# The sum over wavelengths moves from VectorE to GpSimd, and GpSimd's queue is put in another order

## The reference

```python
scores = einsum('bhqd,bhkd->bhqk', Q * m, K * m) * SCALE   # m = cos(phase[w, h]), per wavelength w, head h
scores = scores * cos(KERR * scores * scores)              # KERR = 2.7e-12
attn = softmax(scores, axis=-1)
acc += einsum('bhqk,bhkd->bhqd', attn, V) * iw[w]          # over 16 wavelengths
...
x = layernorm(x + (acc / 16) @ Wo + bo)
gates = top-2 of softmax(x @ router_w + router_b) over 8 experts and a pass-through
x = layernorm(x + sum_e gates[e] * gelu(x @ w1[e]) @ w2[e] + gates[8] * x)
```

## Time and profile before

| | |
|---|---|
| median of 3 runs | 7535.9 us (7534.82 to 7537.15) |
| profiled execution | 7540.05 us, span 7538.4 us |
| mean granted TensorE clock | 0.939 of full speed |
| ScalarE (ACT) | 7184.6 us busy, 95% of the span |
| TensorE (PE) | 5560.1 us, 74% |
| VectorE (DVE) | 5456.0 us, 72% |
| GpSimd (POOL) | 44.4 us, 1% |
| exponentials L522 | 6979.3 us in 2048 instructions |
| reduction L773 | 64 instructions of about 1.9 us |

### The profile page before, as it was taken

One profiled execution on the slowest core, in us unless ns is written; L12 is line 12 of the kernel. 1 busy time (PEld: TensorE's weight loads), 2 busy tenths in 40 slices (PEclk: granted clock), 3 DMA queues, 4 the chain that ended last, 5 costly groups with the idle time before them and its releaser, 6 DMA issues.

```text
span 7538.4 us, 124074 instructions
## 1 busy us (share of the span) xinstructions
PE 5560.1 (74%) x43972; PEld 2013.9 (27%) x43972; DVE 5456.0 (72%) x9488; ACT 7184.6 (95%) x2227; POOL 44.4 (1%) x112
## 2 busy tenths in 40 slices
PE   6767767677777777777777777777777777777777
PEld 2222222222222222222222222222222222222225
DVE  4767677767777777777777777777777777777763
ACT  4999999999999999999999999999999999999992
POOL 0000000000000000000000000000000000000000
PEclk7999999999999999999999999999999999999998
DMA  2000000000000000000000000000000000000000
GB/s 57 4 4 4 2 4 4 3 3 9 28 25 28 17 26 23 19 28 19 29 28 16 25 28 16 26 28 16 28 30 17 26 27 14 28 17 26 27 12 34
DMA packets 40422, 151.80 MB, mean 20 GB/s; under 512 B 7969, under 2 KB 26273, under 8 KB 33441
## 3 DMA queue, kind: packets, MB, share of 16 engines
q1 hardware_dynamic: 39072, 142.13, 5.7%
q0 software_dynamic: 768, 1.57, 0.1%
HBM read 132.66 MB, written 11.01 MB: 19 GB/s over the span
## 4 chain that ended last, share of the span: by engine, by line
ACT 44%; issue 29%; PE 12%; DVE 8%; ACTq 6%; DMA 1%; DVEq 0%; POOLq 0%; SPq 0%; POOL 0%
ACT ring L522 43%; PE pv L593 8%; ACTq L517 4%; DVE scores L724 2%; DMA out<-tile_out 1%; DVE vprobs L747 1%; ACTq L518 1%; DVE tile_z L810 1%; PE sc L1042 1%; PE tr L1050 1%; PE sc L648 1%; DVE qt L718 0%; DVE tile_small L360 0%; DVE tile_small L359 0%; DVE tile_small L361 0%
## 5 line engine op out<-in xcount | busy, mean ns | idle before, releaser
L522 ACT ACTIVATE ring<-scores 128x4096 f32<-128x4096 f32 (+3 forms) x2048 | 6979.3, 3497 | 144.5 <-PE pv L593 109.3
L593 PE MATMUL pv<-ring,vh 128*32 128x512 f32 x31744 | 4010.8, 635 | 1702.1 <-ACT ring L522 1574.4
L593 PEld LDWEIGHTS pv<-ring,vh 128*32 128x32 f32 x31744 | 1003.7, 115 | 4350.8 <-ACT ring L522 2189.0
L754 DVE COPY numer<-pv 128x512 f32<-128x512 f32 x512 | 353.6, 691 | 1067.7 <-PE pv L593 1062.4
L747 DVE SCALAR_TENSOR_TENSOR vprobs<-vprobs,vrest 128x512 f32<-128x512 f32 x1536 | 1063.8, 693 | 52.3
L714 DVE TENSOR_REDUCE rowmax<-sc 128x1 f32<-128x1024 f32 x512 | 602.5, 1219 | 120.8 <-PE sc L556 120.8
L724 DVE COPY scores<-sc 128x1024 f32<-128x1024 f32 (+1 forms) x512 | 601.6, 1217 | 59.0 <-PE sc L575 58.4
L593 PE MATMUL pv<-vprobs,vh 128*32 128x512 f32 x1024 | 530.3, 599 | 0.0
L745 DVE TENSOR_TENSOR vprobs<-vprobs,vrest 128x512 f32<-128x512 f32 x512 | 354.7, 693 | 17.6
L741 DVE SCALAR_TENSOR_TENSOR vrest<-vpower,vrest 128x512 f32<-128x512 f32 x512 | 354.6, 693 | 17.6
L748 DVE SCALAR_TENSOR_TENSOR vprobs<-vprobs,vpower 128x512 f32<-128x512 f32 x512 | 354.5, 692 | 17.4
(11 more groups left out here) (156 smaller groups left out, 2408.2 us busy)
## 6 DMA issues: line engine op xcount, KB each, us to landing
tile_w<-in_L_ffn_w SPq DMA_DIRECT2D x48, 2048.0 KB, 7.6
qt<-q_scratch SPq DMA_DIRECT2D x256, 36.0 KB
kt_<-k_scratch SPq DMA_DIRECT2D x256, 36.0 KB
ring<-in_L_ffn_w SPq DMA_DIRECT2D x2, 2048.0 KB, 11.5
scores<-in_L_attn_x SPq DMA_DIRECT2D x4, 512.0 KB, 4.9
q_scratch<-qt SPq DMA_DIRECT2D x4, 512.0 KB, 3.9
k_scratch<-kt_ SPq DMA_DIRECT2D x4, 512.0 KB, 4.2
v_scratch<-vv SPq DMA_DIRECT2D x4, 512.0 KB, 3.5
```

The source lines that it names most:

```text
L522: nc.scalar.activation(ring[:, i % SLOTS, 0:cols], scores[:, bass.ds(n % 2, 1), half * CK:(half + 1) * CK, :].rearrange("p o k s -> p (o k ...
L593: last = nc.tensor.matmul(pv[g * VC:(g + 1) * VC, pair % 2, :], vh[:, buf, half * CK + k, :], probs, start=(half == 0 and k == 0), stop=(h ...
L754: nc.vector.tensor_copy(numer[:, pair, :], pv[:, pair, :]).then_inc(pv_read, 1)
```

## The change

The reduction of VectorE is removed. In its place GpSimd adds the 8 pairs of wavelengths of `parts` in a tree, in place (4 + 4, 2 + 2, 1 + 1), then the two wavelengths of the pair that is left into a new small tile `att_head`, and copies that into `att`; a semaphore wait stands between the steps. VectorE waits for `head_summed` ahead of the first write to `parts` of the next head, since the tree works in place. On GpSimd's queue a pair of heads n, n+1 is now: copy the values of head n+2, sum head n, store the tile and wait for it, copy the values of head n+3, sum head n+1. The loop's last round is written out, without copies.

```diff
@@ -123,6 +123,7 @@
         coef = sb("coef", [P, 32])
         parts = sb("parts", [P, W // 2, 8, 2, D])
         att = sb("att", [P, KT, E])
+        att_head = sb("att_head", [P, KT, D])
 
 
         tile_w = sb("tile_w", [P, NE * F])
@@ -194,7 +195,7 @@
         def pool_setup(pool):
             for started in (xT_ready, q_made, k_made, v_mm, v_made, peak_made, qkv_stored, probs_ready, tr_full,
                             tr_read, att_made, att_stored, gen_scores, gen_tr, ff_x1, ff_gelu, ff_expert,
-                            ff_added, ff_stored, tile_x1_made, tile_products, tile_added, tile_out_free):
+                            ff_added, ff_stored, tile_x1_made, tile_products, tile_added, tile_out_free, head_summed):
                 pool.sem_inc(started, START)
             nc.gpsimd.memset(numer[0:NH, :, :], 0.0).then_inc(edges_made, 1)
             nc.gpsimd.memset(vprobs[0:NH, :, :], 1.0).then_inc(edges_made, 1)
@@ -426,6 +427,7 @@
         pv_read = sem("pv_read")
         tr_full, tr_read = sem("tr_full"), sem("tr_read")
         norm_step = sem("norm_step")
+        head_step, head_summed = sem("head_step"), sem("head_summed")
 
         tile_in, tile_w1, tile_w2 = sem("tile_in"), sem("tile_w1"), sem("tile_w2")
         tile_attT_ready, tile_attT_made, tile_y = sem("tile_attT_ready"), sem("tile_attT_made"), sem("tile_y")
@@ -484,21 +486,45 @@
             pool.wait_ge(slot_free, NCH * (n - 1) + SLOTS)
             nc.gpsimd.tensor_copy(vh[:, buf, :, 0:D], vv[:, :, bass.ds((n % H) * D, D)]).then_inc(vh_ready, 1)
 
+        def sum_wavelengths(pool, n):
+            pool.wait_ge(tr_read, 4 * (n + 1) + START)
+            apart(pool)
+            for step, left in enumerate((4, 2, 1)):
+                nc.gpsimd.tensor_tensor(parts[:, 0:left], parts[:, 0:left], parts[:, left:2 * left], ALU.add).then_inc(head_step, 1)
+                pool.wait_ge(head_step, 3 * n + step + 1)
+                apart(pool)
+            nc.gpsimd.tensor_tensor(att_head[:, :, :], parts[:, 0, :, 0, :], parts[:, 0, :, 1, :], ALU.add).then_inc(head_summed, 1)
+            pool.wait_ge(head_summed, n + 1 + START)
+            pool.wait_ge(att_stored, 32 * (n // H) + START)
+            apart(pool)
+            nc.gpsimd.tensor_copy(att[:, :, bass.ds((n % H) * D, D)], att_head[:, :, :]).then_inc(att_made, 1)
+
         def pool_main(pool):
             pool.sem_inc(slot_free, SLOTS)
             pool.wait_ge(v_loaded, 16)
             nc.gpsimd.tensor_copy(vh[:, 0, :, 0:D], vv[:, :, 0:D]).then_inc(vh_ready, 1)
             nc.gpsimd.tensor_copy(vh[:, 1, :, 0:D], vv[:, :, D:2 * D]).then_inc(vh_ready, 1)
-            with pool.Fori(1, FIRST_PAIR) as i:
-                copy_values(pool, 2 * i, 0)
-                copy_values(pool, 2 * i + 1, 1)
-            with pool.Fori(0, PAIRS - FIRST_PAIR) as i:
-                copy_values(pool, 2 * (i + FIRST_PAIR), 0)
-                copy_values(pool, 2 * (i + FIRST_PAIR) + 1, 1)
+            with pool.Fori(0, FIRST_PAIR) as i:
+                copy_values(pool, 2 * i + 2, 0)
+                sum_wavelengths(pool, 2 * i)
+                copy_values(pool, 2 * i + 3, 1)
+                sum_wavelengths(pool, 2 * i + 1)
+
+            def tile_heads(i, last=False):
+                n = 2 * (i + FIRST_PAIR)
+                if not last:
+                    copy_values(pool, n + 2, 0)
+                sum_wavelengths(pool, n)
                 pool.wait_ge(tile_done, i + 1)
                 pool.dma_start(out_tiles[bass.ds(i, 1)].rearrange("o p e -> p (o e)"), tile_out[:, :]).then_inc(tile_stored, 16)
                 pool.wait_ge(tile_stored, 16 * (i + 1))
                 pool.sem_inc(tile_out_free, 1)
+                if not last:
+                    copy_values(pool, n + 3, 1)
+                sum_wavelengths(pool, n + 1)
+            with pool.Fori(0, PAIRS - FIRST_PAIR - 1) as i:
+                tile_heads(i)
+            tile_heads(PAIRS - FIRST_PAIR - 1, True)
 
         def scalar_main(act):
             act.preload_act_table(ACT.Exp)
@@ -763,15 +789,11 @@
                                     wl_wide[:, 2 * quad:2 * quad + 2, :, :].rearrange("p a t w -> p (a t w)"),
                                     ALU.mult).then_inc(norm_step, 1)
             dve.wait_ge(norm_step, 8 * n + 2 * quad + 2)
+            if quad == 0:
+                dve.wait_ge(head_summed, n + START)
             nc.vector.tensor_tensor(parts[:, 2 * quad:2 * quad + 2, :, :, :].rearrange("p a t w d -> p (a t w) d"), blocks[:, :, 0:D],
                                     coef[:, :].rearrange("p (g o) -> p g o", o=1).to_broadcast([P, 32, D]),
                                     ALU.mult).then_inc(tr_read, 1)
-
-        def sum_wavelengths(dve, n):
-            dve.wait_ge(tr_read, 4 * (n + 1) + START)
-            dve.wait_ge(att_stored, 32 * (n // H) + START)
-            nc.vector.tensor_reduce(att[:, :, bass.ds((n % H) * D, D)], parts[:, :, :, :, :].rearrange("p a t w d -> p t d a w"),
-                                    axis=AX.XY, op=ALU.add).then_inc(att_made, 1)
 
         def tile_part_one_vector(dve, i, step, then):
             if step == 0:
@@ -853,7 +875,6 @@
                     elif at == 15 and more:
                         exponentials(dve, n + 1, 0)
             normalise(dve, n, 3)
-            sum_wavelengths(dve, n)
 
         def vector_main(dve):
             for t in range(KT):
```

## The result

The changed kernel is slower: a median of 7591.5 us against 7537.2 us for the kernel before in the same series, a ratio of 1.0071 with a 95% interval of [1.0056, 1.0086]. The forecast was 7465 us in a range of 7448 to 7508.

The account below looks back on a forecast made before the run. ScalarE's stream of exponentials was taken to bound the kernel, so only its idle time could be gained: 7540.05 - 86.4 + 11.4 + 4.1 = 7469.2 us, less 4.15 from profiled execution to median, 7465.0 us; range 7448 to 7508.

Parts of the forecast that it names:

- its two gaps: ScalarE's idle places four and twenty exponentials into the even head of tile pairs: 86.4 and 20.0 us in all.
- the start gap: ScalarE's idle time four exponentials into a tile pair's even head, 23 of 24 pairs, 86.4 us, expected to go.
- GpSimd's wait goes in 23 pairs: At pair starts, copying values ahead of the tile's store ends TensorE's wait for GpSimd: -86.4 us.
- this place is clean, with 2.7 to 3 us in hand: At the pair start, nothing else was said to be late once the copies come early; slack 2.7 to 3 us.
- store latency: Pair-start stall read as GpSimd's wait for the tile's store to land, plus the slow clock after idling; 4.00 us at one boundary.
- The second gap, 11.4 us given back: ScalarE's idle time twenty exponentials into the even head grows to a mean of 1.1 us: 22 x 0.52 = 11.4 us lost.
- one of two exceptions: First and last tile pairs before the change lost 3.62 and 3.71 us at twenty exponentials; other 22 lost 0.54 to 0.60.
- Rival A: The stall moves to twenty exponentials, 3.6 us in every pair: 66.9 us given back, 7520 us; chance 0.20.
- The tree at 3.7 us, hidden by 31 us: GpSimd's sum of a head takes 3.7 us and costs nothing, since VectorE needs it only 31 us later.
- rival B: GpSimd's tree and VectorE's exponentials lock each other out of SBUF: 7646 us at 6 us a head; chance 0.04.
- The tail, +4.1 us: Behind the last head, GpSimd's store and tree end at 7374.5 instead of 7370.38: +4.1 us once, bounds +1.8 and +13.
- VectorE's 122 us are worth nothing: Removing 64 reductions of 1.91 us from VectorE gains nothing on ScalarE's stream, as VectorE then waited 2.61 us for TensorE.

Follow-up runs that it names:

- busy_and_cut: Changed kernel with TensorE's loop cut inside the odd head and 36 extra matmuls a pair in TensorE's idle time: 7456.2 us, 0.9894 of the kernel before.
- sum_only: Kernel before with only the tree sum on GpSimd, both copies of values still behind the tile's store: 7541.2 us, 1.0007.
- the last pair of runs: Changed kernel, TensorE's loop cut inside the odd head, router product and ScalarE's small exponential later; with tree 7428.0 us, with VectorE's reduction 7428.9 us.
- numer_first: Changed kernel with VectorE copying a pair's last numerators ahead of the tile's last layer norm: 7484.2 us, 0.9929 of the kernel before.
- loop_cut_moved: Changed kernel with TensorE's jump back moved between steps 3 and 4 of the odd head, where it waits for the GELU: 7536.6 us, 0.9997.
- before_two_pairs: Kernel before with TensorE's loop over pairs written out twice per round: 7556.8 us, 1.0026.

## Why the prediction was wrong

- *That ScalarE's stream bounds, and its two gaps are all there is to gain*: right in the main; without the start gap and with 21.1 us of the second it is 7456.2 us (`busy_and_cut`), and 7428 without either, with the router and its small exponential moved.
- *That GpSimd's wait goes in 23 pairs*: right. *That this gives 86.4 us, for "this place is clean, with 2.7 to 3 us in hand"*: this is the step that failed. Behind the wait lay TensorE's restart, 3.0 to 3.7 us in 22 pairs, and it was 9.7 us, not 86.4, that went. The trace of before had it in full view: the wait list has `PE pv L593 <- issue: 23.3, 7, 3.5`, seven times, once for every jump back in the 16 heads without a tile. The first pair, which has no gap, is entered from the loop ahead without a jump back; its missing gap was explained by the missing store. I took the free moment of an engine for the moment at which it could issue. The rest of the stall was also read too simply: "store latency" was 3.7 to 4.5 us beside the jump and 2.62 in the last pair, where there is none.
- *The second gap, 11.4 us given back*: its direction and its cause, the clock, were right, its size was not: 49.7 us, a mean gap of 2.9 us where 1.1 was put in. Slow batches were put in one pair of six, and came in 17 of 24. The last pair of before, where TensorE stood idle the shortest at the start (2.80 us) and the second gap was 3.71, was a sign of it; it was counted as one of two exceptions. Rival A had 66.9 us, at a chance of 0.20, and the worse half of it outside the range, but never beside start gaps that stay.
- *The tree at 3.7 us, hidden by 31 us*: right, 3.6 us from 7414.25 to 7417.82, and 3.9 with its waits inside the loop; VectorE's wait for it cost nothing, `sum_only` shows it. The factor of two of the Trainium skill ("GPSIMD Engine Reference", section Engine selection) had led to an estimate of 4.6 with the waits, which was less near. Without the waits the five instructions took 3.0 us together, between the 2.5 of my sum and the 3.4 by that factor. VectorE's exponentials did not get longer (L773, 692 ns, against 693 for the same line, L747, before), so rival B falls.
- *The tail, +4.1 us*: +1.8. The store there landed at most 2.3 us after its issue. The 4.05 us of the sum came from a pair start beside TensorE's jump; the tail has no jump.
- *That VectorE's 122 us are worth nothing*: right in `sum_only` and in the last pair of runs (7428.0 and 7428.9 us).

The sum, corrected: 7540.1, less 9.7 at the starts, plus 49.7 at the second place, plus 1.8 for the tail is 7581.9, against 7586.2 measured; 3.4 of the last 4.3 us lie in ScalarE's exponentials themselves (6982.7 against 6979.3).

Open: why the length of the idle time at the start goes with the step that falls to the low clock. That it does is seen in three traces, and that holding the clock takes the loss away is tested; no run set this idle time by itself, and the slow step was not predicted for any of these kernels.

## What to carry to other kernels

Before a wait is priced as a gain, ask what the waiting engine would do at that moment: a loop's jump back costs TensorE 3.0 to 3.7 us here, and a wait that ends later hides it completely. Put an engine's jump where it waits anyway, or let the work ahead of it end earlier, and keep waits of helper work out of the way of the stream that bounds. Where a few tenths of a microsecond of idle time decide which batches run at the low clock, judge a small edit with the clock held too, or its sign may be the clock's.

## What was not expected of the hardware

- TensorE takes 3.0 to 3.7 us from the last instruction of a loop's round to the first product of the next (97.4 us in 29 times in `numer_first`, where it is seen most plainly).
- A shorter idle time at one place went with more idle time at another: with the start gaps at 0 the second gaps were 3.66 us in pair after pair, 87.8 us in all, against 69.7 in the changed kernel and 20.0 in the one before.
- The same store from GpSimd's queue let the next instruction go 3.7 to 4.5 us after its issue beside a jump of TensorE, and 2.5 to 2.8 us after it with the jump moved (`loop_cut_moved`); `before_two_pairs` has both in turn. It is not the jump alone: in `busy_and_cut`, with the jump moved and 36 products a pair added, 17 of 23 took 3.4 to 4.5 us, and that stays open. The Trainium skill, "SBUF — State Buffer", section SBUF: two separate sides, has a DMA from GpSimd's queue wait for its descriptors while VectorE runs an instruction in a two-port mode. That does not explain the difference here, since VectorE's exponentials stand beside the store in both cases.
